# Sixteen-head attention with two heads in the halves of TensorE's rows, row and column scores side by side

## The chip, the cores and the metric

One core of one Trainium2 chip runs the whole program. The metric is the device time of one execution in microseconds (us); the kernel before took 780.82 us (median of 3 runs, 778.27 to 783.65). TensorE is called PE here, VectorE DVE, ScalarE ACT, GpSimd POOL and SyncE SP.

## The reference

Four layers, each an attention over a context and then a feed-forward part, every one added to `x` (8 batches of 256 tokens, 128 wide) after a layer norm:

```
x = x + L0_xattn(norm(x), ctx)   # att0: 8 heads of 16
x = x + L0_ffn(norm(x))          # ffn0: mixes each token with the one before it
x = x + L1_xattn(norm(x), ctx)   # att1: 16 heads of 8, then relu(out @ W1 + b1) @ W2 + b2
x = x + L1_ffn(norm(x))          # moe1: 8 experts, top 2
x = x + L2_xattn(norm(x), ctx)   # att2: 8 heads of 16
x = x + L2_ffn(norm(x))          # moe2
x = x + L3_xattn(norm(x), ctx)   # att3: one head
x = x + L3_ffn(norm(x))          # moe3: 8 experts, top 2, and a shared one
```

The change is in att1. Per batch and head it computes

```
scores = einsum("bnhd,bmhd->bhnm", q, k) / sqrt(8)       # 256 x 256 for each of 16 heads
out    = einsum("bhnm,bmhd->bnhd", softmax(scores), v)
h      = relu(out @ W1 + b1);  y = h @ W2 + b2
```

## The kernel before

Each engine has its own instruction stream, written out in order; semaphores alone tie them together, so an engine that waits holds up all that is written behind it. att0, ffn0 and att1 form one pipeline ("flow") over batches. A step of the flow has one batch in each role: `p` gets its queries and keys, `m` its row scores and maxima, `a` its column scores, exponentials and averages, `d` its output chain. Steps that hold an att1 batch in `m`, `a` or `d` have 16 **beats**. Tables of numbers say in which beat a piece is issued (`COL_BEAT`, `VALUE_BEAT`, `CHAIN_BEATS`, `SORT_STEPS` and so on).

Queries and keys are split into three bf16 parts, and SP copies them by DMA into a **stack**: for a head, the partitions hold the products of parts that are to be summed (`SLOTS`: nine products of 8 dimensions make 72 partitions in att1, padded to 96). A head's 256 x 256 scores are computed twice on PE, each time by two matmuls of 256 columns:

- `rows` (L2076): queries down the partitions; DVE takes each query's maximum (`negmax`, L952).
- `columns` (L2088): keys down the partitions; three more partitions of the stack carry the negative maxima, so that ACT (L1732) can take the exponential straight from PSUM.

Between them, for one batch: POOL splits the maxima in three (L1474 and on), PE turns them (`turn_max`, L2117), ACT copies them (`maxt`, L1798), and SP writes them into the stack by DMA (L787); the columns wait for that. `averages` (L2104) multiplies the exponentials of four heads by the values, four tiles of 32 columns of the array at a time; ACT copies the result (`nd`, L1737), PE turns it (`turn_averages`, L2128), DVE divides (L921, L924), PE turns that (`turn_o`, L2058), ACT copies it (`ot`, L1747), PE computes the hidden layer (L2171), ACT its relu (L1754), PE the output (L2202), and DVE adds it to `x` (L934). Three stacks are used in turn, so a batch's stack is written again three batches later.

In att1's steps each beat issues the columns of one head of `a`, then the rows of one head of `m`; other pieces of PE work stand between beats. From the last step on, pieces of moe1's routing for tiles 0 to 7 stand between them too (`SORT_STEPS["moe1"]`). moe1 then runs its 46 tiles of 128 tokens, about 1.45 us each.

Of the kernel before, what the change touches and what calls it, by code (L numbers as in the profile page):

```python
# [32 lines left out]
P = 128  # L33
B = 8
# [19 lines left out]
MAXROW = 96  # L54


# [34 lines left out]
def part_tiles(g):  # L91
# [13 lines left out]
    "moe1": {"stats": ((-1, 3), (2, 3)), "rstd": ((-1, 4), (2, 4)), "norm": ((-1, 8), (2, 6)),  # L105
             "turn": ((-1, 10), (-1, 12), (2, 13), (2, 15)), "turned": ((-1, 11), (-1, 13), (3, 0), (3, 1)),
             "logits": (-1, 15), "top": (0, 1), "pick": (0, 4), "mark": (0, 6), "exp": (0, 7), "rank": (0, 8),
             "place": (0, 9), "weigh": (1, 12), "load": (2, 6), "logits2": (3, 3)},
# [4 lines left out]
SEND_FROM = {"moe1": 12, "moe2": 7}  # L113
# [27 lines left out]
COL_BEAT = {8: 3, 16: 6}  # L141
GROUP_LAG = 5
VALUE_BEAT = 4
NORM_BEAT = {8: 4, 16: 7}
PLACE_BEAT = {8: 5, 16: 7}


MIX_BEATS = {"stats": (5, 5), "rstd": (6, 6), "norm": (7, 10), "turn": (3, 5), "turned": (4, 6), "rk": (6, 10), "gate": (7, 11),
             "gated": (5, 6), "mixed": (6, 7)}


CHAIN = ("turn", "finish", "turn_o", "ot", "proj", "hid", "proj2", "residual")
CHAIN_BEATS = {8: (1, 2, 4, 5, 6, None, None, 7), 16: (1, 2, 4, 5, 6, 7, 9, 10)}
# [131 lines left out]
def build(nc, args, out):  # L285
# [3 lines left out]
    with ExitStack() as ctx:  # L289
# [6 lines left out]
        stack_in = [ctx.enter_context(nc.semaphore(f"stack_in{i}")) for i in range(3)]  # L296
        maxrow_in = [ctx.enter_context(nc.semaphore(f"maxrow_in{i}")) for i in range(3)]
        const_ready = ctx.enter_context(nc.semaphore("const_ready"))
        maxrow_ones = ctx.enter_context(nc.semaphore("maxrow_ones"))
        rows_padded = ctx.enter_context(nc.semaphore("rows_padded"))  # L300
# [88 lines left out]
        def lists_of(s):  # L389

            return stack[buf("att" + s[3:], B - 3)]
# [75 lines left out]

        def batch_at(flow, g):

            stages = FLOWS[flow]  # L470
            last = B * len(stages)
            if g < 0:
                return stages[0], g
            return (stages[g // B], g % B) if g < last else (stages[-1], B + g - last)

        def steps_of(flow):
# [3 lines left out]
            last = B * len(FLOWS[flow])  # L480
            at = lambda g: batch_at(flow, g)
            for g in range(last + 4):
                p, m, a, d, n = (at(g - lag) for lag in (0, 1, 2, 3, -1))
                heads = max([H[s] for s, b in (m, a, d) if valid(b)], default=8)
# [22 lines left out]
        def group_beats(s):  # L507
            return [GROUP * j + COL_BEAT[H[s]] + GROUP_LAG for j in range(H[s] // GROUP)]

# [3 lines left out]
        def chain(link):  # L513


            def beats(s):
                k = CHAIN_BEATS[H[s]][CHAIN.index(link)]
                return [] if k is None or (s != "att1" and link in ("hid", "proj2")) else [region_beats(s)[-1] + k - H[s]]
            return beats

        def region_beats(s):
            per = H[s] // GROUP // REGIONS
            return [k + 1 for k in group_beats(s)[per - 1::per]]
# [73 lines left out]
        def uses(s, b):  # L597

            return [st for st in ATT for i in range(B)
                    if buf(st, i) == buf(s, b) and (ATT.index(st), i) <= (ATT.index(s), b)]  # L600

        def stack_total(s, b):

            return sum(16 * len(SLOTS[st]) for st in uses(s, b))
# [66 lines left out]
        def maxrow_total(s, b):  # L671
            return 16 * len(uses(s, b))
# [5 lines left out]
        def _(sp):  # L678
# [70 lines left out]
            def spread_heads(s, p):  # L749

                nh, dh, i = H[s], D // H[s], buf(s, p)
                if s == "att1" and p < 3:
                    sp.wait_ge(rows_padded, p + 1)
                    sp.wait_ge(rows_filled, 3)
                if (s, p) == EARLY:
                    wait(sp, "experts_ready", "moe1", 0)
                wait(sp, "cols_psum", s, p - 3)
                for j, (qa, kc) in enumerate(SLOTS[s]):
                    if j == 0:
                        wait(sp, "qk0_ready", s, p)  # L760
                    if j == 1:
                        wait(sp, "qk1_ready", s, p)
                    if j == 4:
                        wait(sp, "qk2_ready", s, p)
                    n = len(SLOTS[s])
                    sp.dma_start(stack[i][j:j + n * (dh - 1) + 1:n, 0:nh, :, :],
                                 qk_parts[:, qa:3 + kc + 1:3 + kc - qa, :]).then_inc(stack_in[i], 16)
# [1790 lines left out]
```

## Time and profile before

| | |
|---|---|
| median of 3 runs | 780.82 us |
| the profiled execution | 789.78 us |
| its span, first to last instruction | 788.0 us |
| busy: PE, DVE, ACT, POOL | 644.8, 483.9, 395.6, 303.8 us |
| row scores of att1, first to last batch (DVE's maxima) | 131.0 to 289.4 us |
| column scores of att1 end (ACT's exponentials) | 308.4 us |

Read the stretch from 131 to 308 us as nine steps of 18 to 23 us, each with one batch's 16 heads. In the timeline the column "idle before" says how long the engine had nothing running before the group, and what released it. Matmuls overlap one another: a matmul that lasts 0.27 us by its record can be followed by the next one 0.11 us after its start. So the distance from start to start is what a group costs PE, not its busy time.

### The profile page before, as it was taken

To read this page: it belongs to the slowest core of one execution; us is meant where nothing else is said; L and a number is where in the kernel's file an instruction comes from. 1 tells how busy PE (TensorE), PEld (TensorE's weight loads), DVE (VectorE), ACT (ScalarE), POOL (GpSimd) and SP (SyncE) were. 2 spreads that over 40 slices of the span, in tenths; PEclk is the share of its full clock that TensorE was granted. 3 is DMA by queue.
4 is the path that set the end of the run, shared out by engine and by line. 5 is a ranking of instruction groups with operands and counts; after the bars stand their busy time and mean duration, and the time that the engine had idled before them with its cause. 6 is when DMAs were issued, how large, how long until landed. Compare 5 with 4: busy or idle time off the path is not lost.

```text
span 788.0 us, 15312 instructions
## 1 busy us (share of the span) xinstructions
PE 644.8 (82%) x4712; PEld 471.8 (60%) x4712; DVE 483.9 (61%) x1396; ACT 395.6 (50%) x892; POOL 303.8 (39%) x456
## 2 busy tenths in 40 slices
PE   2698887899998887899977787747898677699997
PEld 1355665566665544799944555427787566356655
DVE  4567765877678553555867775636657655455543
ACT  5356574466666455466624655425676454132221
POOL 4435455433323036162756744372545730000000
PEclk9999999999999899699976998857999999699999
DMA  6254423333333100144354441012344200223331
GB/s 177 61 136 105 124 70 90 96 107 88 88 96 86 52 19 35 49 135 115 105 138 122 114 120 43 15 41 80 119 138 141 75 11 1 69 63 102 100 96 56
DMA packets 93575, 68.52 MB, mean 87 GB/s; under 512 B 9800, under 2 KB 84424, under 8 KB 93272
## 3 DMA queue, kind: packets, MB, share of 16 engines
q1 hardware_dynamic: 89400, 59.15, 26.9%
q0 software_dynamic: 4096, 8.40, 3.5%
q8 instruction: 40, 0.66, 0.4%
q14 instruction: 39, 0.32, 0.1%
HBM read 30.75 MB, written 14.35 MB: 57 GB/s over the span
## 4 chain that ended last, share of the span: by engine, by line
PE 35%; DVE 9%; issue 6%; DMA 5%; POOL 3%; ACT 2%; SPq 0%; DVEq 0%; ACTq 0%; POOLq 0%
PE ps L2389 6%; PE ps L2399 4%; PE ps L2427 4%; PE ps L2429 4%; PE ps L2440 4%; DMA late<-outputs_moe,placed 2%; DVE negmax L952 2%; PE ps L2076 1%; POOL gathered L1575 1%; PE ps L2028 1%; PE ps L2383 1%; PE ps L2104 1%; PE ps L2088 1%; DVE x_sb L1270 1%; POOL rstd L1441 1%
## 5 line engine op out<-in xcount | busy, mean ns | idle before, releaser
L952 DVE TENSOR_REDUCE negmax<-ps 128x2 f32<-128x512 f32 x256 | 169.2, 686 | 100.6 <-PE ps L2076 99.7
L1732 ACT ACTIVATE exps<-ps 128x512 f32<-128x512 f32 x256 | 148.9, 599 | 102.2 <-PE ps L2088 100.8
L2076 PE MATMUL ps<-stack 96*128 96x256 bf16 x512 | 103.7, 297 | 26.5 <-DVE negmax L952 22.6
L2088 PE MATMUL ps<-stack 99*128 99x256 bf16 x512 | 101.2, 288 | 19.8 <-DMA stack<-maxt 18.7
L1575 POOL DMA_INDIRECT gathered<-z,placed x64 | 62.6, 978 | 66.8 <-PE ps L2383 28.5
L2088 PEld LDWEIGHTS ps<-stack 99*128 99x128 bf16 x512 | 44.1, 102 | 62.1 <-DMA stack<-maxt 25.1
L1593 POOL DMA_INDIRECT late<-outputs_moe,placed x64 | 62.1, 971 | 49.2 <-PE ps L2383 14.8
L2076 PEld LDWEIGHTS ps<-stack 96*128 96x128 bf16 x512 | 48.6, 104 | 52.1 <-DVE negmax L952 38.5
L2104 PE MATMUL ps<-exps,values 128*32 128x256 f32 x1024 | 75.5, 413 | 1.2 <-ACT exps L1732 1.0
L1977 ACT ACTIVATE gated<-ps 128x512 f32<-128x512 f32 x36 | 21.5, 597 | 83.4 <-PE ps L2429 83.4
L2399 PE MATMUL ps<-pack_moe,ht 128*128 x368 | 59.4, 285 | 1.5 <-DVE y_kept L1357 0.6
L1377 DVE TENSOR_TENSOR ht<-ps,gated 128x512 f32<-128x512 f32 x36 | 24.9, 692 | 45.2 <-ACT gated L1977 45.1
L2399 PEld LDWEIGHTS ps<-pack_moe,ht 128*128 128x128 f32 x368 | 49.1, 194 | 4.6 <-issue 3.1
L2389 PE MATMUL ps<-gated,exps 128*128 128x128 f32 x368 | 51.1, 284 | 0.1
L2440 PEld LDWEIGHTS ps<-pack_moe,ht 128*128 128x128 f32 x288 | 38.2, 195 | 20.3 <-issue 13.4
L2389 PEld LDWEIGHTS ps<-gated,exps 128*128 128x128 f32 x368 | 47.1, 200 | 0.6 <-issue 0.4
L2104 PEld LDWEIGHTS ps<-exps,values 128*32 128x32 f32 x1024 | 30.7, 114 | 21.3 <-issue 9.3
L2440 PE MATMUL ps<-pack_moe,ht 128*128 128x128 f32 x288 | 39.3, 280 | 3.2 <-DVE ht L1377 3.2
L2427 PE MATMUL ps<-stack,pack_moe 128*128 128x512 f32 x64 | 33.8, 611 | 7.0 <-DVE stack L1400 7.0
L1520 POOL TENSOR_TENSOR qk_rest<-qk,qk_parts 128x512 f32<-128x512 f32 x24 | 27.7, 1154 | 29.9 <-DVE qk_parts L963 29.9
L2429 PE MATMUL ps<-stack,pack_moe 128*128 128x512 f32 x64 | 33.6, 607 | 0.0
L1963 ACT ACTIVATE ht<-ps,pack_moe 128x128 f32<-128x128 f32 x92 | 28.7, 364 | 9.5 <-PE ps L2399 6.9
(224 smaller groups left out, 1267.5 us busy)
## 6 DMA issues: line engine op xcount, KB each, us to landing
stack<-qk_parts SPq DMA_DIRECT2D x168, 128.0 KB
stack<-weights_t SPq DMA_DIRECT2D x32, 256.0 KB, 3.3
outputs_moe<-y_kept SPq DMA_DIRECT2D x92, 64.0 KB
ht<-gathered SPq DMA_DIRECT2D x44, 128.0 KB, 2.2
pack_moe<-in_moe SPq DMA_DIRECT2D x11, 256.5 KB, 3.9
pack_moe<-in_moe SPq DMA_DIRECT2D x6, 429.5 KB
gathered<-y_kept SPq DMA_DIRECT2D x10, 256.0 KB, 3.4
pack_moe<-in_moe SPq DMA_DIRECT2D x1, 1732.0 KB, 7.4
```

What stands on the lines that cost most here:

```text
L952: dve.tensor_reduce(negmax_of[b % 2][:, :, h:h + 1].rearrange("p t h -> p (t h)"), ps[:, h % 2, :].rearrange("p (t k) -> p t k", t=2), AX, ...
L1575: pool.indirect_dma_start(gathered[g], at, z[:, t, :], None).then_inc(sent[i], 16)
L1593: pool.indirect_dma_start(back[:, n, :], None, averaged[s, g], at).then_inc(back_in[n], 16)
L1732: nc.scalar.activation(exps[:, i, :], ps[:, 2 + h % 2, :], ACT.Exp, scale=scale)\
L2076: last = pe.matmul(ps[:, h % 2, t * T:(t + 1) * T], st[0:MAXROW, h, 0, t * P:(t + 1) * P], st[0:MAXROW, h, 1, :], start=True, stop=True)
L2088: last = pe.matmul(ps[:, 2 + h % 2, t * T:(t + 1) * T], st[0:MAXROW + 3, h, 1, t * P:(t + 1) * P], st[0:MAXROW + 3, h, 0, :], start=True, ...
L2104: last = pe.matmul(ps[STRIP * k:STRIP * (k + 1), AV, r * T:(r + 1) * T], values[nh][:, buf(s, a), kt, u, :], exps[:, slot(s, a, u), kt * T ...
L2389: last = pe.matmul(ps[:, (j + 1) % 2, c * P:(c + 1) * P], up_kept[s][:, (j + 1) % 2, c * P:(c + 1) * P], taken_t[:, (j + 1) % 2, :], start ...
L2399: last = pe.matmul(ps[:, 3 + (j - 1) % 2, 0:D], turned[:, (j - 1) % 2, c * P:(c + 1) * P], par(s, "experts")[:, bass.ds(at + (up_width(s) ...
L2427: pe.matmul(ps[:, 2 * (i % 2), :], par(s, "w1")[:, w * P:(w + 1) * P], rhs, start=True, stop=True)
L2429: pe.matmul(ps[:, 2 * (i % 2) + 1, :], par(s, "w3")[:, w * P:(w + 1) * P], rhs, start=True, stop=True).then_inc(sem["up_psum"], 1)
L2440: last = pe.matmul(ps[:, 4 + blk % 2, t * D:(t + 1) * D], ht[:, q % 2, 0, t * P:(t + 1) * P], par(s, "w2")[:, w * P:(w + 1) * P], start=(q ...
```

## The change

What it does, part by part:

1. att1's stack keeps six of the nine products: 48 partitions a head. Even heads lie in partitions 0 to 47, odd heads in 64 to 111, and their three rows of maxima behind them. The matmuls of rows and columns thereby use tiles of 64 rows of the array (half the array) in place of all 128 rows. One of SP's DMAs serves one half, so there are 12 of 64 KB per batch instead of 9 of 128 KB, and two for the maxima instead of one.
2. In each beat that has a column head and a row head of att1, which then lie in different halves, PE issues column, row, column, row (`rows_beside_columns`), after both waits.
3. `COL_BEAT` of att1 goes from 6 to 8. Averages come in two halves in two neighbouring beats, and so do hidden layer and output; the output chain's beats are further apart, and it ends 8 beats later. The values' matmul goes from beat 4 to 12.
4. A fourth home for att1's stacks: a head pair needs one slot, so the third stack holds two batches.
5. The padding changes: POOL's three clears of the stack (L1544) go; ACT writes ones into the unused partitions in two smaller pieces per home, for the fourth home in att1's third step, beat 10; ACT writes the ones of the maxima's rows (`fill_ones`) for 8 head slots instead of 16, and a fourth time at moe1's tile 5.
6. moe1's routing of the first tiles comes later: its statistics go from beat 3 to beat 11 of the step with tail -1, its places from beat 9 to beat 12 of the next.

```diff
-    "att1": [(0, 0), (0, 1), (1, 0), (1, 1), (0, 2), (2, 0), (1, 2), (2, 1), (2, 2)],
+    "att1": [(0, 0), (0, 1), (1, 0), (1, 1), (0, 2), (2, 0)],
-MAXROW = 96
+MAXROW = {"att0": 96, "att1": 48, "att2": 96}
+HALF = P // 2
+HALVES = {"att0": 1, "att1": 2, "att2": 1}
...
-    "moe1": {"stats": ((-1, 3), (2, 3)), "rstd": ((-1, 4), (2, 4)), "norm": ((-1, 8), (2, 6)),
+    "moe1": {"stats": ((-1, 11), (2, 11)), "rstd": ((-1, 12), (2, 12)), "norm": ((-1, 14), (2, 15)),
...
-COL_BEAT = {8: 3, 16: 6}
-GROUP_LAG = 5
-VALUE_BEAT = 4
+COL_BEAT = {8: 3, 16: 8}
+GROUP_LAG = {8: 5, 16: 6}
+GROUP_BEATS = {8: 1, 16: 2}
+VALUE_BEAT = {8: 4, 16: 12}
...
-CHAIN = ("turn", "finish", "turn_o", "ot", "proj", "hid", "proj2", "residual")
-CHAIN_BEATS = {8: (1, 2, 4, 5, 6, None, None, 7), 16: (1, 2, 4, 5, 6, 7, 9, 10)}
+CHAIN = ("turn", "finish", "turn_o", "ot", "proj", "proj_b", "hid", "proj2", "proj2_b", "residual")
+CHAIN_BEATS = {8: (1, 2, 4, 5, 6, None, None, None, None, 7), 16: (1, 2, 5, 5, 8, 9, 10, 12, 13, 14)}
...
+        def home(s, b):
+            if s == "att1":
+                return 3 + b % HOMES, stack[min(b % HOMES, 2)], 8 * (b % HOMES < 3)
+            return buf(s, b), stack[buf(s, b)], 0
...
+            def spread_slot(s, p, j):
+                nh, dh, (i, st, first), n = H[s], D // H[s], home(s, p), len(SLOTS[s])
+                qa, kc = SLOTS[s][j]
+                for half in range(HALVES[s]):
+                    at = half * HALF + j
+                    sp.dma_start(st[at:at + n * (dh - 1) + 1:n, first:first + nh // HALVES[s], :, :],
+                                 qk_parts[half::HALVES[s], qa:3 + kc + 1:3 + kc - qa, :]).then_inc(stack_in[i], 16)
...
-                            wait(pool, "cols_psum", s, p - 3)
-                            pool.memset(stack[buf(s, p)][0:MAXROW, 0:8, 1, :].bitcast(F32), 0.0).then_inc(rows_padded, 1)
...
+            def row_half(s, m, h, t):
+                (at, k), (_, st, first) = half_place(s, h), home(s, m)
+                st = st[at:at + MAXROW[s], first + k, :, :]
+                return pe.matmul(ps[:, h % 2, t * T:(t + 1) * T], st[:, 0, t * P:(t + 1) * P], st[:, 1, :], start=True, stop=True)
...
+            def rows_beside_columns(s, a, h, m, g):
+                wait_columns(s, a, h)
+                wait_rows(s, m, g)
+                for t in range(2):
+                    column = column_half(s, a, h, t)
+                    row = row_half(s, m, g, t)
+                column.then_inc(sem["cols_psum"], 1)
+                row.then_inc(sem["rows_psum"], 1)
...
-                for kt in range(2):
+                for kt in halves:
...
+                if [st for st, _, _ in col + row] == ["att1", "att1"] and (col[0][2] + row[0][2]) % 2:
+                    rows_beside_columns(*col[0], *row[0][1:])
```

PE's stream in the middle of att1, where averages, `turn_o` and the hidden layer stand between the beats. Before (L2088 columns, L2076 rows, L2104 averages of four heads, L2058 `turn_o`, L2171 hidden layer):

```order
L2104 MATMUL ps<-exps,values16 32x256 x8
L2088 MATMUL ps<-stack2 128x256 x2
L2076 MATMUL ps<-stack0 128x256 x2
L2058 MATMUL ps<-pack_consts,o 128x128 x2
L2088 MATMUL ps<-stack2 128x256 x2
L2076 MATMUL ps<-stack0 128x256 x2
L2088 MATMUL ps<-stack2 128x256 x2
L2076 MATMUL ps<-stack0 128x256 x2
L2171 MATMUL ps<-ot,pack_att1 128x256 x2
```

The same place in the changed kernel (L2146 columns, L2133 rows, L2184 averages, L2197 `turn_max`, L2203 hidden layer):

```order
L2184 MATMUL ps<-exps,values16 32x256 x4
L2146 MATMUL ps<-stack2 128x256
L2133 MATMUL ps<-stack1 128x256
L2146 MATMUL ps<-stack2 128x256
L2133 MATMUL ps<-stack1 128x256
L2197 MATMUL ps<-ident16,negmax_parts 48x128 x2
L2184 MATMUL ps<-exps,values16 32x256 x4
L2146 MATMUL ps<-stack2 128x256
L2133 MATMUL ps<-stack1 128x256
L2146 MATMUL ps<-stack2 128x256
L2133 MATMUL ps<-stack1 128x256
L2203 MATMUL ps<-ot,pack_att1 128x256
```

Columns and rows now alternate matmul by matmul, and in such a step a piece of other work follows every beat's four matmuls, where before some beats followed one another with nothing between.

The same stream where the averages' last group of a batch is followed by `turn_averages`, which needs ACT's copy of it. Before (L2128 `turn_averages`):

```order
L2104 MATMUL ps<-exps,values16 32x256 x8
L2088 MATMUL ps<-stack1 128x256 x2
L2076 MATMUL ps<-stack2 128x256 x2
L2088 MATMUL ps<-stack1 128x256 x2
L2076 MATMUL ps<-stack2 128x256 x2
L2128 MATMUL ps<-pack_consts,nd 128x128 x4
```

In the changed kernel (L2277 values, L2219 `turn_averages`):

```order
L2184 MATMUL ps<-exps,values16 32x256 x4
L2146 MATMUL ps<-stack2 128x256
L2133 MATMUL ps<-stack0 128x256
L2146 MATMUL ps<-stack2 128x256
L2133 MATMUL ps<-stack0 128x256
L2277 MATMUL ps<-pack_att1,ctxt_sb 128x128 x2
L2146 MATMUL ps<-stack2 128x256
L2133 MATMUL ps<-stack0 128x256
L2146 MATMUL ps<-stack2 128x256
L2133 MATMUL ps<-stack0 128x256
L2219 MATMUL ps<-pack_consts,nd 128x128 x4
```

Two beats lie between as before, with the values' matmuls now among them.

SP's stream in one step of att1. Before (L787 the maxima of one batch, L766 the stack of the next but one, L730 and L695 loads for later):

```order
L787 DMA stack1<-maxt 3x16x256
L766 DMA stack0<-qk_parts 8x32x256 x5
L766 DMA stack0<-qk_parts 8x16x512
L766 DMA stack0<-qk_parts 8x32x256 x3
L730 DMA gathered_1<-y_kept 128x4x128
L695 DMA pack_moe<-in_moe1 128x513
```

In the changed kernel (L814 maxima, L781 stack):

```order
L781 DMA stack0<-qk_parts 8x16x256 x2
L814 DMA stack2<-maxt 3x8x256 x2
L781 DMA stack0<-qk_parts 8x16x256 x8
L781 DMA stack0<-qk_parts 8x8x512 x2
L756 DMA gathered_1<-y_kept 128x4x128
L721 DMA pack_moe<-in_moe1 128x513
```

Two DMAs of the stack now stand ahead of the maxima, and 14 DMAs take the place of 10.

## Rows read from the trace of the kernel before

**Rows 1.** The page, part 1: busy time, share of the span, instructions.

```profile
span 788.0 us, 15312 instructions
PE 644.8 (82%) x4712; PEld 471.8 (60%) x4712; DVE 483.9 (61%) x1396; ACT 395.6 (50%) x892; POOL 303.8 (39%) x456
```

**Rows 2.** Windows by att1's steps: busy us and instructions of each engine, PE clock.

```profile
core 0: us, PE busy (x) PEld busy (x) DVE busy (x) ACT busy (x) POOL busy (x), PEclk, DMA share, GB/s
131.00:149.20 18.20, 16.68 (x142) 11.51 (x139) 14.43 (x34) 8.80 (x23) 6.34 (x10) 0.91 0.35 97
149.20:168.30 19.10, 15.89 (x131) 10.51 (x132) 14.07 (x35) 9.87 (x25) 8.72 (x17) 1.00 0.33 92
168.30:188.00 19.70, 17.97 (x170) 12.33 (x168) 14.09 (x32) 13.51 (x32) 7.54 (x15) 1.00 0.33 89
188.00:207.80 19.80, 18.78 (x178) 13.35 (x178) 13.45 (x27) 13.55 (x33) 6.65 (x13) 1.00 0.32 89
225.90:243.90 18.00, 16.31 (x160) 10.96 (x159) 12.38 (x23) 12.22 (x28) 4.47 (x9) 1.00 0.30 82
243.90:267.30 23.40, 20.48 (x178) 13.78 (x177) 15.83 (x45) 13.22 (x29) 5.95 (x9) 0.90 0.26 67
267.30:289.40 22.10, 18.41 (x161) 11.50 (x161) 15.96 (x42) 10.69 (x24) 4.25 (x8) 0.88 0.09 26
289.40:308.40 19.00, 14.20 (x144) 7.72 (x143) 4.88 (x24) 13.36 (x27) 11.51 (x18) 1.00 0.10 37
```

**Rows 3.** Timeline of PE in one step: start, us, line, shape, [idle before <- releaser].

```profile
...
193.54 0.38 PE L2076 MATMUL ps<-stack 96*128 96x256 bf16 x2
193.76 0.38 PE L2088 MATMUL ps<-stack 99*128 99x256 bf16 x2
193.98 0.38 PE L2076 MATMUL ps<-stack 96*128 96x256 bf16 x2
194.29 1.07 PE L2104 MATMUL ps<-exps,values 128*32 128x256 f32 x16
195.30 0.39 PE L2088 MATMUL ps<-stack 99*128 99x256 bf16 x2
...
206.31 0.59 PE L2144 MATMUL ps<-zt,pack_att 128*128 128x256 f32 x2
206.75 0.60 PE L2145 MATMUL ps<-ctxt_sb,pack_att 96*128 96x256 f32 x2
```

**Rows 4.** Timeline of PE, cut at 194.53 us: the first four matmuls of a group.

```profile
194.29 0.42 PE L2104 MATMUL ps<-exps,values 128*32 128x256 f32 x4
```

**Rows 5.** Waits from 188 to 244 us: engine, line, releaser: us, times, longest.

```profile
PE ps L2088 <- DMA stack<-maxt: 1.6, 3, 0.9
...
PE ps L2171 <- ACT ot L1747: 1.2, 3, 0.4
PE ps L2128 <- ACT nd L1737: 1.2, 3, 0.4
```

**Rows 6.** The same view from 243.9 to 289.4 us.

```profile
PE ps L2076 <- DVE negmax L952: 2.4, 3, 1.0
PE ps L2088 <- DMA stack<-maxt: 2.3, 2, 1.4
PE ps L2171 <- ACT ot L1747: 1.0, 2, 0.8
```

**Rows 7.** Timeline of SP's queue in the same step.

```profile
190.51 0.77 SPq L787 DMA_DIRECT2D stack<-maxt  x1
192.24 6.41 SPq L766 DMA_DIRECT2D stack<-qk_parts  x9
```

**Rows 8.** Groups by line, whole span: ACT's fills.

```profile
L1678 ACT ACTIVATE stack<-zt 32x2048 f32<-32x2048 f32 x3 | 5.7, 1906 | 0.1
L1685 ACT ACTIVATE stack<-neghalf 3x2048 f32<-3x2048 f32 x3 | 5.5, 1893 | 0.0
```

**Rows 9.** Timeline of PE around the end of att1.

```profile
294.52 0.61 PE L2088 MATMUL ps<-stack 99*128 99x256 bf16 x4 [1.72 <-DMA stack<-maxt]
...
326.99 0.23 PE L2355 MATMUL ps<-picks,upper 128*128 128x64 bf16 x1 [1.50 <-DVE picks L1217]
```

More of the change, by code:

```diff
@@ L389, in lists_of @@
         def lists_of(s):
[L391 removed]
+            return home("att" + s[3:], B - 3)[1]
         picks16 = sb("picks16", [P, len(PART[0]), E], BF16)
@@ L476, in steps_of @@
         def steps_of(flow):
-            last = B * len(FLOWS[flow])
+            stages = FLOWS[flow]
+            last = B * len(stages)
             at = lambda g: batch_at(flow, g)
@@ L764, in spread_heads, with place_maxima @@
                         wait(sp, "qk2_ready", s, p)
-                    n = len(SLOTS[s])
-                    sp.dma_start(stack[i][j:j + n * (dh - 1) + 1:n, 0:nh, :, :],
-                                 qk_parts[:, qa:3 + kc + 1:3 + kc - qa, :]).then_inc(stack_in[i], 16)
+                    spread_slot(s, p, j)
+            def spread_heads(s, p):
+                spread_first(s, p)
+                spread_rest(s, p)
+            def place_maxima(s, m):
+                wait(sp, "maxt_ready", s, m)
+                wait(sp, "cols_psum", s, freed(s, m))
+                i, st, first = home(s, m)
+                for half in range(HALVES[s]):
+                    at = half * HALF + MAXROW[s]
+                    sp.dma_start(st[at:at + 3, first:first + H[s] // HALVES[s], 0, :], maxt[half:3 * H[s]:HALVES[s], :])\
+                        .then_inc(maxrow_in[i], 16)
             for flow in FLOWS:
@@ new lines, in wait_columns, with column_half @@
+            def wait_columns(s, a, h):
+                if h == 0:
+                    pe.wait_ge(maxrow_in[home(s, a)[0]], maxrow_total(s, a))
+                    pe.wait_ge(maxrow_ones, min(a + 1, 3) if s == "att0" else 3 if s == "att1" else 4)
+                wait(pe, "exp_ready", s, a, h - 2)
+            def column_half(s, a, h, t):
+                (at, k), (_, st, first) = half_place(s, h), home(s, a)
+                st = st[at:at + MAXROW[s] + 3, first + k, :, :]
+                return pe.matmul(ps[:, 2 + h % 2, t * T:(t + 1) * T], st[:, 1, t * P:(t + 1) * P], st[:, 0, :], start=True, stop=True)
@@ L2113, in turn_max @@
                 wait(pe, "placed_ready", "moe1", 0, 0) if (s, m) == ("att1", B - 1) else None
-                wait(pe, "route_exp_in", "moe1", 0, 0) if (s, m) == ("att1", B - 2) else None
                 rows_of = 3 * H[s]
@@ L2119, in turn_max, with find_hidden, find_output @@
                 last.then_inc(sem["maxt_psum"], 1)
+            def find_hidden(s, c):
+                return pe.matmul(ps[:, TURN, c * T:(c + 1) * T], par(s, "w1")[:, c * P:(c + 1) * P], ot[:, :], start=True, stop=True)
+            def find_output(s, t):
+                for c in range(2):
+                    last = pe.matmul(ps[:, ND, (2 + t) * D:(3 + t) * D], hid[:, c, t * P:(t + 1) * P],
+                                     par(s, "w2")[:, c * P:(c + 1) * P], start=(c == 0), stop=(c == 1))
+                return last
             def turn_averages(s, d):
@@ L2152, in beat @@
                     wait(pe, "qk_ready", s, p)
+                    wait(pe, "hid_ready", sd, d - 1) if sd == "att1" and valid(d - 1) else None
                 if u == mix_at("turn", heads) and f2 is not None:
@@ L2215, in beat @@
                     wait(pe, "qk_ready", s, p)
+                    wait(pe, "hid_ready", sd, d - 1) if sd == "att1" and valid(d - 1) else None
                     wait(pe, "val_ready", "ffn0", f2) if f2 is not None else None
@@ L2236, in beat @@
                 for st, b, j in due(flow, step, u, "a", group_beats):
-                    averages(st, b, j)
+                    averages(st, b, j, range(3 - GROUP_BEATS[H[st]]))
+                for st, b, j in due(flow, step, u, "a", later_halves):
+                    averages(st, b, j, (1,))
             def attention(flow):
```

196 lines of the change are left out of this document (107 added, 89 removed).

## The prediction

> **What bounds the kernel now.** I read the page's first part, then the windows by step, then PE's timeline inside one step, then the waits, and last the end of att1.
>
> PE is busy 82% of the span and no other engine over 61% [rows 1], but that is a mean over different stages. The windows cut att1 at its steps [rows 2]. In the four steady steps, from 168.3 to 243.9 us, a step takes 18.0 to 19.8 us; PE is busy for 16.3 to 18.8 of it, DVE for 12.4 to 14.1 and ACT for 12.2 to 13.6, at the full clock (2.4 GHz). So PE bounds them, with some 4 us of room to the next engine. From 243.9 to 289.4 the steps are longer, 23.4 and 22.1 us, with a granted clock of 0.90 and 0.88 and DVE at 16: routing work of moe1 stands in them. In the last step, columns only, ACT has 13.4 of 19.0.
>
> The timeline gives what PE pays [rows 3]. Groups of two score matmuls start 0.22 us apart, so one costs 0.11 us, and a step's 64 of them 7.0 us. A step has four groups of averages; a group's 16 matmuls take 1.01 us to the next one's start. Two float32 matmuls of 256 columns over the whole array take 0.44 us, 0.22 each, and so 16 of them would take 3.5; four averages in the four column strips fit into 0.42 us by their records [rows 4]. So tiles of the array do run beside one another here, for columns. Entering such a group costs extra: the last rows start at 193.98, are done with their 0.22 at 194.20, and the averages start at 194.29, which makes **0.09 us** per change of tile shape. Leaving may cost 0.13 (1.01 less four times 0.22), but that rests on a modelled pitch.
>
> The waits of three steady steps are few [rows 5]: 1.6 us for the maxima's DMA, 1.2 each for `ot` and `nd`, 4.0 us in all, 1.3 a step. In the two longer steps they are 2.3 for the DMA, 1.0 for `ot` and 2.4 for DVE's maxima [rows 6].
>
> **The change, part by part.**
>
> *Halves.* In a beat with a column and a row head, four matmuls in sequence (0.44 us) become two pairs. If the halves run beside each other, a pair costs 0.11 and the beat 0.22: a gain of 0.22 x 16 = 3.5 us per steady step. No tile of 64 rows stands in this trace; the two bounds are 0.22 us per beat (like the strips) and 0.44 (like two whole-array matmuls). I take 0.22, since the nearest row is that of the strips.
>
> *Changes of tile shape.* Before, a step entered and left a special shape four times, 8 changes. After, each of 16 beats' pairs is followed by work of another shape, 32 changes: 24 more. At 0.09 us that is +2.2 us a step. The bounds are 0 (half rows need no change) and 0.13 each, +3.1.
> The Trainium skill, "TensorEngine Tiling (Array Packing)", section Key Properties, says that changing the tiling mode, not just the tile, drains TensorE. The 0.09 us fits it for column strips, and no row here shows it for halves. It speaks against this change, since the beats were spread apart by other work.
>
> *Waits.* Columns now come 5 beats after the turn of the maxima instead of 3, and `turn_averages` and the hidden layer stand further from what they need: the 1.3 us a step go [rows 5]. SP works longer for this: a maxima DMA occupies its queue for 0.77 us and nine of the stack 6.41, 0.71 each [rows 7]. Fourteen at 0.71 to 0.77 are 9.9 to 10.8 us, two of them ahead of the maxima; this fits into a step of 16 us, so I cost it at nothing. If it did not fit, the maxima would be late and the columns would wait as in the last step now, 1.72 us [rows 9]. The joint wait of a pair is new: row and column now stand still if either DVE or ACT is late. In the steady steps PE waits for neither at a score matmul [rows 5]. With the steps shorter I take +0.5, between 0 and the 1.3 just removed.
>
> A steady step: -3.5 + 2.2 - 1.3 + 0.5 = **-2.1 us**, four of them -8.4.
>
> *The two longer steps.* The same, with 3.3 us of DMA and `ot` waits in two steps, 1.65 each, in place of 1.3 [rows 6]: -3.5 + 2.2 - 1.65 + 0.5 = -2.45 each, **-4.9**. Routing now has 17 beats in place of 22; if DVE's waits of 2.4 us double, half of this is lost, and if they go it is -7.3.
>
> *Before and after the steady steps.* From 149.2 to 168.3 nine beats are paired: 9 x 0.22 = 2.0 saved, up to 18 more changes x 0.09 = 1.6 paid. ACT has to write the fourth home, as the fills of 1906 ns a piece [rows 8], but is busy for only 9.9 of 19.1 us; I take +0.1 and call the step **-0.3**. From 131.0 to 149.2 the rows of att1 in halves stand alone among att0's columns over the whole array: no pair, some 14 round trips of 0.18, +2.5. PE has 1.5 us idle there, part of which takes it: **+2.0** (0 to 2.5). In the last step the columns start two beats later, about 1.7 us by its 0.85 a beat (columns and two groups of averages in a step of 19.0 us over 22 beats), and the DMA wait of 1.72 goes [rows 9]; in halves and alone, they also pay changes: **+0.5**. From there to routing's rank matmul at 326.99, which waits for DVE's picks [rows 9], and on to moe1, the chain's steps are the same. At moe1's tile 5 ACT writes ones for 8 slots; half of 1893 ns [rows 8] on a chain from PE through ACT, bounds 0 and 0.95: **+0.5**. POOL's clears free POOL, which bounds nothing here. The filling of the homes at the start lies beside loads: 0.
>
> Sum: -8.4 - 4.9 - 0.3 + 2.0 + 0.5 + 0.5 = **-10.6**, say -10 us. The profiled execution took 789.8 us, so it would take 780; the median of the runs shown is 780.8, 9 us below the profiled one, and the forecast for a median is **771 us**.
>
> **The rivals.** A measurement of this kernel can tell about 1% from no change, here 773.0 to 788.6.
>
> *Halves cost no change of shape.* Then 24 x 0.09 = 2.2 us more are gained in six steps, 13 us, and 2 in the step at 131: **756 us**. For it: rows and columns both use all 128 columns, so the output side does not change. Against it: the gap seen before averages. By the skill's rule named above this rival falls away; a gap of 0.09 us ahead of strips is the only row that bears on it.
>
> *The saved time goes back to DVE and ACT.* Each head passes through DVE once and ACT once, both take other work between, and two buffers of scores each (the remainder of the head by two) are all that stands between them and PE. If pairs wait for both, the six steps keep their length, the step at 131 pays its 2: **781 us**, no change. For it: DVE's 12.4 to 14.1 busy plus lumps of other work in one beat. Against it: 4 us of room per step [rows 2], and the lumps are split.
>
> *Slower: the halves run one after another.* The place is the pair. If its second matmul waits for the first, 105 beats (6 x 16 + 9) cost 0.44 in place of 0.22 while the changes are paid: 105 x 0.22 = 23 us more than forecast, **793 us**. It decides from a price per beat of 0.22 + 10/105 = 0.32 us on. For it: no tile of 64 rows in the trace. Against it: the strips of the averages [rows 4].
> The Trainium skill, "TensorE: Matmul & The Clock Gate", Part 3, gives a measured speedup of 3.07 for four row tiles of 32 rows; by it this rival falls. No row here shows row tiles.
>
> **How the numbers follow.** Forecast (765 to 777): 0.46. No cost of shape: 0.22. Back to DVE and ACT: 0.15. One after another: 0.13. The rest, 0.04, is a collapse of the order, such as SP late for every step. The range takes in the forecast, the second rival with 7 us above it, up to 788, and the first rival with 2 below it, down to 754; outside lie the serial halves, the rest and what of the first rival gains more. Faster by over 1% needs less than 773: some two thirds of the forecast's own range (0.31) and the first rival, 0.53. Within 1%: the forecast's other third and the second rival, 0.32. Slower: 0.15.
>
> **What would show it.** In the changed profile's timeline of PE the second matmul of a pair starts about 0.01 us after the first, and two pairs are 0.11 us apart; starts 0.11 us apart within a pair mean serial halves. A gap of 0.09 us or so ahead of and behind each beat's pairs shows the changes of shape; without it the first rival is right. The steady steps should last 16 to 17.7 us, PE still with the fewest idle time, no wait of columns on the maxima's DMA, of `turn_averages` on `nd` or the hidden layer on `ot`. If instead pairs wait for `negmax` or `exps` in most beats, the second rival is right. The forecast is wrong too if SP's maxima land after the columns' beat, if the granted clock falls in the steady steps, or if routing's places come so late that moe1 starts later than att1's end allows.

## The result and the profile after

The changed kernel takes **792.26 us** (median of 4 runs, 788.16 to 793.07), the kernel before 782.24. The ratio is 1.0106 (95% interval 1.0071 to 1.0141), so it is slower by 1.1%, where 10 us less had been forecast; 792 also lies outside the range. A second series gave 1.0092 (1.0056 to 1.0128).

PE is busy for 651.0 us, 82% of the span, and the other engines are within 3 us of what they were [rows 1].

The kernel before was profiled once more, in an execution of 786.29 us, nearer its median than the one that the prediction rests on. Its windows, by stretches of steps (start and end in us, their length, busy us and instructions of PE, PE's weight loads, DVE, ACT and POOL, PE's granted clock as a share of 2.4 GHz, DMA share, GB/s):

```profile
128.00:146.20 18.20, 16.73 (x142) 11.59 (x140) 14.56 (x35) 8.87 (x23) 6.40 (x10) 0.91 0.36 98
146.20:165.20 19.00, 15.87 (x130) 10.50 (x131) 13.98 (x35) 9.78 (x25) 8.62 (x17) 1.00 0.33 92
165.20:240.80 75.60, 69.95 (x667) 48.23 (x665) 53.33 (x109) 51.98 (x119) 24.71 (x46) 1.00 0.32 88
240.80:286.30 45.50, 38.89 (x337) 25.29 (x336) 31.79 (x86) 23.91 (x52) 10.20 (x16) 0.89 0.18 47
286.30:305.30 19.00, 14.17 (x144) 7.69 (x142) 4.86 (x24) 13.34 (x27) 11.49 (x18) 1.00 0.10 37
305.30:398.70 93.40, 84.19 (x685) 79.59 (x685) 56.98 (x214) 50.24 (x110) 42.96 (x48) 0.93 0.35 99
```

The same stretches of the changed kernel, which answer to [rows 2] (the fourth line is a part of the third, its last three steps):

```profile
126.20:155.20 29.00, 23.71 (x142) 11.78 (x142) 14.99 (x35) 9.56 (x24) 6.04 (x9) 0.76 0.18 47
155.20:174.60 19.40, 18.55 (x112) 10.37 (x112) 14.17 (x33) 10.46 (x23) 7.34 (x14) 0.65 0.26 69
174.60:243.00 68.40, 65.60 (x659) 31.13 (x656) 53.53 (x109) 51.70 (x115) 26.48 (x49) 1.00 0.28 74
191.70:243.00 51.30, 50.05 (x497) 23.47 (x497) 39.32 (x78) 39.13 (x87) 18.85 (x35) 1.00 0.27 72
243.00:288.00 45.00, 40.17 (x339) 18.76 (x342) 32.14 (x86) 24.75 (x53) 9.37 (x16) 0.77 0.14 38
288.00:308.40 20.40, 18.86 (x166) 7.55 (x167) 3.31 (x10) 15.84 (x33) 12.41 (x17) 1.00 0.10 38
308.40:407.00 98.60, 86.96 (x692) 82.32 (x690) 58.69 (x226) 51.30 (x111) 42.61 (x49) 0.90 0.33 94
```

Read the length, the number behind the two ends of each line, against its partner. The sums are 270.7 and 280.8 us. The two profiled spans differ by less, 784.5 and 789.7. One reason stands just ahead of the first stretch, which begins with att1's first maximum. In the first profile PE's line there was

```profile
130.52 0.39 PE L2076 MATMUL ps<-stack 96*128 96x256 bf16 x2 [2.65 <-DMA stack<-qk_parts]
```

(2.40 us in the second): att1's first rows waited for the DMA of their stack. In the changed kernel this wait is gone. From att0's last rows to att1's first maximum it takes 6.2 us (120.02 to 126.19) where the kernel before took 8.6 (119.36 to 128.00), so 2.5 us were gained that no term of the forecast had. What took the wait away was not tried; it stays away in the runs below. The other reason is that this execution was 3.1 us shorter behind moe1, where the change has no part.

| stretch | forecast | measured |
|---|---|---|
| ahead of the first step, rows' wait for their stack | 0 | -2.5 |
| first step, rows of att1 beside att0's columns | +2.0 | **+10.8** |
| second step, 9 beats paired | -0.3 | +0.4 |
| four steady steps | -8.4 | **-7.2** |
| two steps with routing | -4.9 | -0.5 |
| columns only | +0.5 | +1.4 |
| end of att1 and moe1 | +0.5 | **+5.2** |
| sum | -10.6 | +7.6 |

The steady steps do most of what was forecast. The loss stands in the first step and behind att1; the two steps with routing gain almost nothing.

Two rows of the table compare unequal work, since columns, averages and the output chain now come some beats later. The second step has 112 of PE's matmuls in place of 130, and the first of the steady steps lacks a hidden layer and an output; later steps take this over, the columns-only step with 166 in place of 144. The last three steady steps hold the same work in both kernels: they went from 55.9 us (188.0 to 243.9 in [rows 2]) to 51.3, which is 1.5 us a step.

**The steady steps.** PE's timeline in the changed kernel, beside [rows 3] (L2146 columns, L2133 rows; columns: start, us, line, shape, count):

```profile
208.04 0.27 PE L2146 MATMUL ps<-stack 51*128 51x256 bf16 x1
208.04 0.27 PE L2133 MATMUL ps<-stack 48*128 48x256 bf16 x1
208.24 0.64 PE L2184 MATMUL ps<-exps,values 128*32 128x256 f32 x8
208.81 0.28 PE L2146 MATMUL ps<-stack 51*128 51x256 bf16 x1
...
208.93 0.27 PE L2146 MATMUL ps<-stack 51*128 51x256 bf16 x1
```

Column and row start together, and the next pair 0.12 us later: four score matmuls cost 0.23 us where two took 0.22 before. The averages start 0.20 after the last pair, 0.09 more than its 0.11; eight of them, two groups of four at 0.22, take 0.57 to the next pair, 0.13 more than 0.44. So each change of shape costs about 0.1 us in both directions. The Trainium skill, "TensorEngine Tiling (Array Packing)", section Key Properties, has this drain on a change of tiling mode, and the trace agrees. With float32 work of the whole array between the pairs it is more: four matmuls of L2277 stand at 205.41, 0.20 after the last pair, and the next pair at 206.05, 0.64 later, where the same four took 0.44 before (191.38 to 191.82). That makes 0.29 us for entering and leaving, against 0.22 with averages.

The waits of PE from 175 to 243 us, four steps, beside [rows 5] (line, releaser: us, times, longest):

```profile
PE ps L2146 <- DVE negmax L998: 1.3, 3, 0.7
...
PE ps L2146 <- ACT exps L1781: 0.3, 1, 0.3
```

The waits for the maxima's DMA, `nd` and `ot` are gone; pairs wait for DVE and ACT 1.6 us in four steps, 0.4 a step where 0.5 was taken. The line left out is 1.1 us of idle time ahead of L2253 in two steps, which the profile puts down to no wait ("issue").

**The first step.** PE's wait there; before, columns waited 0.55 us here:

```profile
131.31 0.46 PE L2146 MATMUL ps<-stack 99*128 99x256 bf16 x2 [4.24 <-DMA stack<-maxt]
```

SP's queue (start, us) shows why, beside [rows 7]:

```profile
127.30 1.62 SPq L781 DMA_DIRECT2D stack<-qk_parts  x2
129.02 0.77 SPq L814 DMA_DIRECT2D stack<-maxt  x1
```

and DVE and ACT what SP's two entries needed:

```profile
124.68 0.37 ACT L1849 ACTIVATE maxt<-ps 24x256 bf16<-24x256 bf16 x1
126.80 0.42 DVE L1009 CAST qk_parts<-qk 128x512 bf16<-128x512 f32 x1
```

The maxima of att0's last batch were ready at 125.05. They were sent at 129.02, because SP stood at the two stack parts written ahead of them, and these need DVE's cast, done at 127.22. The columns waited 4.24 us for that. In the same place the clock falls (windows of 4 us; PEclk stands behind POOL's count):

```profile
132.00:136.00 4.00, 4.00 (x26) 1.82 (x24) 2.20 (x5) 1.00 (x2) 0.00 (x0) 0.50 0.38 100
...
140.00:144.00 4.00, 4.00 (x24) 2.25 (x26) 2.48 (x6) 1.69 (x4) 0.00 (x0) 0.50 0.00 0
```

PE is idle from 127.1 to 131.3, and from 132 to 144 it runs at 1.2 GHz although it is busy all the time.

**The end.** PE behind att1's last averages, beside [rows 9] (brackets: idle before, and what ended it; L2072 turns moe1's normed tiles, L2203 is the hidden layer, L2082 routing's logits, L2208 the output, L2458 the rank):

```profile
314.61 0.85 PE L2072 MATMUL ps<-pack_consts,z 128*128 128x128 f32 x6 [2.01 <-DVE z L944]
315.32 1.56 PE L2203 MATMUL ps<-ot,pack_att 128*128 128x256 f32 x4
316.67 2.57 PE L2082 MATMUL ps<-pack_moe,zt 128*128 128x8 f32 x12
319.09 2.06 PE L2208 MATMUL ps<-pack_att,hid 128*128 128x128 f32 x8
...
330.18 0.23 PE L2458 MATMUL ps<-picks,upper 128*128 128x64 bf16 x1 [1.49 <-DVE picks L1263]
```

The last hidden layer stands behind a turn that waits 2.01 us for DVE, and the output behind twelve logits matmuls of 2.4 us. From the last averages (309.02) to the rank it is 21.2 us; before, 18.5.

### The profile page after: what moved, and what is told of

It is laid out like the page before. It is cut to its first block, busy times and chain, and to the rows that moved or that the text cites. A ratio compares the mean times of both kernels' runs of the same rounds, so it can differ in the third digit from the quotient of the medians.

```text
span 789.7 us, 15455 instructions
## 1 busy us (share of the span) xinstructions
PE 651.0 (82%) x4712; PEld 445.5 (56%) x4712; DVE 484.4 (61%) x1396; ACT 398.0 (50%) x898; POOL 301.5 (38%) x453
## 4 chain that ended last, share of the span: by engine, by line
PE 33%; DVE 9%; issue 6%; DMA 4%; POOL 4%; ACT 3%; SPq 1%; DVEq 0%; ACTq 0%; POOLq 0%
PE ps L2492 6%; PE ps L2530 4%; PE ps L2532 4%; PE ps L2543 4%; PE ps L2502 3%; POOL gathered L1617 2%; DVE negmax L998 2%; DMA late<-outputs_moe,placed 2%; PE ps L2082 1%; DVE x_sb L1316 1%; PE ps L2133 1%; PE ps L2184 1%; PE ps L2146 1%; PE ps L2486 1%; PE ps L2385 1%
## 5 line engine op out<-in xcount | busy, mean ns | idle before, releaser
L2133 PE MATMUL ps<-stack 96*128 96x256 bf16 (+1 forms) x512 | 106.7, 306 | 22.7 <-DVE negmax L998 20.9
L2146 PE MATMUL ps<-stack 99*128 99x256 bf16 (+1 forms) x512 | 103.5, 294 | 19.9 <-DMA stack<-maxt 15.5
L2146 PEld LDWEIGHTS ps<-stack 99*128 99x128 bf16 (+1 forms) x512 | 38.0, 100 | 82.6 <-issue 39.0
L2184 PE MATMUL ps<-exps,values 128*32 128x256 f32 x1024 | 81.9, 415 | 0.2 <-issue 0.2
L2133 PEld LDWEIGHTS ps<-stack 96*128 96x128 bf16 (+1 forms) x512 | 39.4, 102 | 46.2 <-DVE negmax L998 34.8
L2530 PE MATMUL ps<-stack,pack_moe 128*128 128x512 f32 x64 | 33.9, 611 | 6.9 <-DVE stack L1446 6.9
L2184 PEld LDWEIGHTS ps<-exps,values 128*32 128x32 f32 x1024 | 27.0, 113 | 22.0 <-issue 15.6
L1511 POOL TENSOR_TENSOR xb<-x_sb,pack_att 128x256 f32<-128x256 f32 x24 | 16.2, 673 | 59.4 <-DVE x_sb L980 38.0
```

The source lines that it names most:

```text
L2133: return pe.matmul(ps[:, h % 2, t * T:(t + 1) * T], st[:, 0, t * P:(t + 1) * P], st[:, 1, :], start=True, stop=True)
L2146: return pe.matmul(ps[:, 2 + h % 2, t * T:(t + 1) * T], st[:, 1, t * P:(t + 1) * P], st[:, 0, :], start=True, stop=True)
L2184: last = pe.matmul(ps[STRIP * k:STRIP * (k + 1), AV, r * T:(r + 1) * T], values[nh][:, buf(s, a), kt, u, :], exps[:, slot(s, a, u), kt * T ...
L2530: pe.matmul(ps[:, 2 * (i % 2), :], par(s, "w1")[:, w * P:(w + 1) * P], rhs, start=True, stop=True)
```

## The experiments

Times are medians; the ratio is that to the kernel before in the same series, and across series it is the safer reading.

**The kernel before again.** No edit.

> The kernel before once more, for a trace beside those of the others. If the profile that the prediction rests on is typical, the maxima of att1's first batch begin near 131 us and its last exponential ends near 308 us, and the granted clock is at its lower level for some 14 us between 120 and 310 us; a whole time near 782 us would then say that the 8 us between the profiled 789.8 us and the median lie behind att1.

786.29 us in one run. Its windows are shown above. Its stretches of att1 are as long as in the first profile to 0.1 us, so the rows that the prediction rests on were typical; what the first profiled execution took longer lay elsewhere. The whole time was not near the 782 us that the expectation names.

**SP's order.**

```diff
-                    if spreads and sm == "att1":
+                    if spreads and sa == "att1":
                         spread_first(s, p)
                     if valid(a):
                         place_maxima(sa, a)
                     if spreads:
-                        spread_rest(s, p) if sm == "att1" else spread_heads(s, p)
+                        spread_rest(s, p) if sa == "att1" else spread_heads(s, p)
```

> The changed kernel, but in the one step that has att0's last batch in role a, SP copies its maxima ahead of the next batch's first stack part. Theory A (a wait and no more): PE's 4.24 us wait at 127 us goes down to about 0.5 and the time falls by 3 to 4 us against the changed kernel's 792, to about 788.5. Theory B (the idle time also brings the clock down, which halves the 13.65 us behind it): the stretch at the lower clock from 131.5 us goes as well and the time falls by 8 to 11 us, to about 783. Theory C (matmuls on half the rows hold the clock down by themselves): the wait goes, the clock falls at 131 or soon behind it all the same, and the time is about 789.

778.91 us, ratio 0.9939 (0.9905 to 0.9973): 13 us less than the changed kernel, above the 8 to 11 of theory B, so theories A and C are too small by far. PE's wait, and the windows of the first two steps:

```profile
129.55 0.39 PE L2146 MATMUL ps<-stack 99*128 99x256 bf16 x2 [0.36 <-DMA stack<-maxt]
```

```profile
128.30:147.50 19.20, 17.81 (x142) 9.75 (x142) 14.69 (x34) 9.46 (x24) 6.05 (x9) 1.00 0.27 71
147.50:166.30 18.80, 17.65 (x112) 10.23 (x112) 14.17 (x33) 10.47 (x23) 7.34 (x14) 0.73 0.27 72
```

The wait is 0.36 in place of 4.24, and the step 19.2 us in place of 29.0, at the full clock. Of the 9.8 us, 3.9 are the wait. What goes beyond theory B lies mainly in the two steps with routing, 42.1 us here where the changed kernel had 45.0.

**The wait kept, but filled.** In the changed kernel, ahead of the same wait:

```diff
+                if (s, a, h) == ("att0", B - 1, 0):
+                    wait(pe, "exp_ready", s, a, h - 2)
+                    for i in range(72):
+                        pe.matmul(ps[:, 2 + h % 2, 0:P], ident16[:, :], ident16[:, :], start=True, stop=True)
                 if h == 0:
                     pe.wait_ge(maxrow_in[home(s, a)[0]], maxrow_total(s, a))
```

> The changed kernel (792 us) with SP's order as it is, so with the wait of 4.24 us for the maxima; but ahead of that wait PE runs 72 extra matmuls of 128 columns on the whole array, 4.0 us by 0.055 each, whose results are overwritten. Nothing that the kernel needs comes earlier. If the idle time is what brings the clock down at 131.5 us, the 13.65 us at the lower level go and the time falls by 4 to 9 us, to 783 to 788. If half rows bring the clock down by themselves, or if the loss was the wait alone, it stays at 790 to 794.

780.64 us, ratio 0.9973 (0.9935 to 1.0010), against 791.21 of the changed kernel in the same series (ratio 1.0092): 10.6 us less by the medians, 9.3 by the ratios, where 4 to 9 were expected, with 72 matmuls more and nothing sooner. The extra work in PE's timeline, and the window of the step:

```profile
127.97 4.19 PE L2140 MATMUL ps<-ident 128*128 128x128 bf16 x72
```

```profile
127.20:149.90 22.70, 21.71 (x214) 13.72 (x213) 14.62 (x34) 9.37 (x24) 6.05 (x9) 1.00 0.22 59
```

The step takes 22.7 us: 3.5 more than with the maxima first, and 6.3 less than with the wait left empty. So the 29.0 us divide into 19.2 for the step, 3.5 for the wait, and 6.3 for the clock that fell at its end. The second step is 1.7 us shorter too, 17.7 us at a granted clock of 0.81 against 19.4 at 0.65.

**The changed kernel again**, in the series of the filler. No edit.

> The changed kernel once more, beside the run with the filler: 789 to 793 us, with the wait of some 4.2 us near 127 us and the lower clock behind it.

791.21 us, as expected.

**The end of att1.** Two edits of `SORT_STEPS["moe1"]`, first on top of the maxima first, then alone:

```diff
-             "turn": ((-1, 15), (0, 2), (3, 2), (3, 3)), "turned": ((0, 0), (0, 3), (3, 3), (3, 4)),
+             "turn": ((-1, 15), (0, 2), (3, 6), (3, 7)), "turned": ((0, 0), (0, 3), (3, 7), (3, 8)),
...
-             "place": (0, 12), "weigh": (1, 12), "load": (2, 6), "logits2": (3, 6)},
+             "place": (0, 12), "weigh": (1, 12), "load": (2, 6), "logits2": (3, 10)},
```

> As the run with the maxima first, and besides the turns of moe1's tiles 8 to 13 stand behind att1's last hidden layer on PE (beats 6 and 7 of the last step instead of 2 and 3), and their logits behind its output (beat 10 instead of 6). If these two insertions are what lengthened the end of att1, the rank matmul comes 3 to 4 us sooner behind the last averages, and the time falls by 3 to 5 us more against the run before it. If the end was longer for the clock alone, nothing changes.

774.00 us, ratio **0.9864** (0.9825 to 0.9904), 4.9 us less than the run before it. PE at the end of att1:

```profile
305.04 1.10 PE L2203 MATMUL ps<-ot,pack_att 128*128 128x256 f32 x4 [0.66 <-ACT ot L1796]
306.40 0.85 PE L2072 MATMUL ps<-pack_consts,z 128*128 128x128 f32 x6 [0.26 <-DVE z L944]
307.08 1.14 PE L2208 MATMUL ps<-pack_att,hid 128*128 128x128 f32 x8
...
317.27 0.24 PE L2458 MATMUL ps<-picks,upper 128*128 128x64 bf16 x1 [1.50 <-DVE picks L1263]
```

The twelve logits matmuls follow the output (at 308.08). From the last averages (300.80) to the rank it is now 16.5 us, 4.7 less than in the changed kernel and 3.8 less than in the run before it (297.86 to 318.11). Part of the 4.7 is the clock again: the output's eight matmuls take 1.14 us here and 2.06 there.

> The changed kernel with only the turns of moe1's tiles 8 to 13 and their logits moved behind the hidden layer and the output. If the two repairs are independent, this one is worth what it was behind the other, 778.9 - 774.0 = 4.9 us: 785 to 789. If the end of att1 is only hurt by the clock, 790 to 793.

784.56 us, ratio 1.0011 (0.9982 to 1.0041), against 791.21 in the same series: 6.7 us less, 6.3 by the ratios. The two repairs add up: 13.1 and 6.3 us alone by the ratios, 18.9 together.

**The order of a pair.** In the changed kernel:

```diff
                 for t in range(2):
                     column = column_half(s, a, h, t)
+                for t in range(2):
                     row = row_half(s, m, g, t)
```

> The changed kernel with column, column, row, row in each paired beat instead of column, row, column, row; waits and all else unchanged. If matmuls of different halves run beside each other only when they are neighbours in the stream, two matmuls of one half follow each other at 0.11 us and the neighbours in the middle overlap: a beat costs 0.33 in place of 0.22 us, 105 beats 11.6 us, of which a part is covered by waits for DVE: 797 to 804 us. If the halves gained nothing, 792.

790.05 us, ratio 1.0100 (1.0062 to 1.0138): no difference to the changed kernel. That is the number of the theory that halves gain nothing, and still not its proof, for the matmuls overlapped all the same. The stream holds column, column, row, row; the trace shows

```profile
207.84 0.28 PE L2146 MATMUL ps<-stack 51*128 51x256 bf16 x1
207.85 0.28 PE L2133 MATMUL ps<-stack 48*128 48x256 bf16 x1
207.96 0.27 PE L2146 MATMUL ps<-stack 51*128 51x256 bf16 x1
207.97 0.27 PE L2133 MATMUL ps<-stack 48*128 48x256 bf16 x1
```

The first row starts beside the first column and 0.11 us ahead of the second column, which stands before it in the stream. By these records each half works through its own matmuls. The Trainium skill, "TensorE: Matmul & The Clock Gate", Part 3, says that matmuls start and end in the order of the program; these starts differ from it, and the records decide here.

**Column and row in the same half**, on the kernel of 774.00 us:

```diff
-COL_BEAT = {8: 3, 16: 8}
+COL_BEAT = {8: 3, 16: 9}
```

> The kernel of the run with the turns late (774.0 us), with att1's columns one beat later (COL_BEAT 9 in place of 8), so that the column head and the row head of a beat lie in the same half of the rows. Every tile, wait and change of shape is as before; only the matmuls cannot run beside each other. The theory that this is where the gain comes from: a beat costs 0.44 us in place of 0.22, 105 beats 23 us, less what waits cover, so 785 to 797 us, and the steady steps last about 3 us longer. If the gain comes from the shorter waits alone: 774 to 776.

832.84 us, ratio 1.0626 (1.0587 to 1.0666). PE's timeline at the full clock, and the windows of the first steady step and of all four:

```profile
207.42 0.39 PE L2146 MATMUL ps<-stack 51*128 51x256 bf16 x2
207.65 0.38 PE L2133 MATMUL ps<-stack 48*128 48x256 bf16 x2
```

```profile
166.60:186.10 19.50, 17.86 (x163) 9.62 (x164) 14.31 (x32) 12.68 (x29) 7.09 (x12) 1.00 0.26 70
166.60:263.20 96.60, 90.26 (x659) 47.05 (x660) 53.82 (x109) 52.27 (x115) 25.64 (x47) 0.82 0.20 52
```

The two heads of a beat cost 0.23 us and the same again, as forecast for serial halves. The step at full clock is 19.5 us where the changed kernel has 17.1 for the same batch (174.6 to 191.7), 2.4 more. The time rises by 59 us, not by up to 23. The rest stands where the clock is lower: the four steady steps take 96.6 us at a granted clock of 0.82 where the kernel of 774.00 us has 68.4 at 1.00, and the mean over the profiled execution is 0.866 against 0.921. What brings it down in the steady steps was not tried; waits for `nd` and `exps` of up to 0.7 us stand there.

**A change of shape more.** On the kernel of 774.00 us, and the control with `ident16` cut to the half of the row head:

```diff
                 for t in range(2):
+                    if t:
+                        pe.matmul(ps[:, g % 2, T:T + 8], ident16[0:P, :], ident16[0:P, 0:8], start=True, stop=True)
                     column = column_half(s, a, h, t)
```

> The same kernel (774.0 us) with one extra matmul of 8 columns on the whole array between the two pairs of each of the 105 paired beats; its result is overwritten. If a change of tile shape costs about 0.09 to 0.13 us each, two more per beat cost 19 to 27 us, less what waits cover: 787 to 801 us, and the two pairs of a beat start 0.35 us apart in place of 0.11. If halves need no change of shape, only the matmul itself counts, some 0.03 to 0.05 us a beat: 777 to 779.

813.42 us, ratio 1.0372 (1.0328 to 1.0416), 39 us more where 13 to 27 were expected. The timeline:

```profile
207.43 0.28 PE L2133 MATMUL ps<-stack 48*128 48x256 bf16 x1
207.64 0.18 PE L2167 MATMUL ps<-ident 128*128 128x8 bf16 x1
207.75 0.28 PE L2146 MATMUL ps<-stack 51*128 51x256 bf16 x1
```

> The control: the same extra matmul of 8 columns, but on the half of the array in which the beat's row head lies, so without a change of tile shape. Both theories: 0.03 to 0.05 us a beat, 777 to 779 us.

785.66 us, with runs from 771.02 to 792.09: by its whole time this decides nothing. The timeline does, and the windows of the four steady steps, first on the whole array, then on the half:

```profile
208.36 0.27 PE L2146 MATMUL ps<-stack 51*128 51x256 bf16 x1
208.36 0.17 PE L2168 MATMUL ps<-ident 64*128 64x8 bf16 x1
208.39 0.27 PE L2133 MATMUL ps<-stack 48*128 48x256 bf16 x1
```

```profile
165.30:246.90 81.60, 80.37 (x723) 42.48 (x722) 54.21 (x109) 52.50 (x115) 25.81 (x48) 0.98 0.23 62
164.40:233.80 69.40, 66.89 (x724) 37.15 (x720) 53.91 (x109) 51.77 (x115) 26.89 (x48) 1.00 0.28 73
```

On the whole array the small matmul puts the pairs 0.32 us apart in place of 0.11, so two changes cost 0.21 with it. On the half it delays its row by 0.03. That is the price that the forecast had. The steady steps, 68.4 us without the extra matmul, bear it out: on the whole array they take 13.2 us more, 3.3 a step, as 16 beats at 0.21 give; on the half 1.0 more. The time of the first run beyond 105 x 0.21 = 22 us lies behind them: its two steps with routing take 52.8 us at a granted clock of 0.69, where the kernel of 774.00 us has 45.0 at 0.77, and the stretch from there to moe1's end 126.5 at 0.82 against 113.6 at 0.95.

**Filler in the rows' step**, on the kernel of 774.00 us:

```diff
                     for st, b, h in row:
+                        if st == "att1" and not col:
+                            wait_rows(st, b, h)
+                            for i in range(6):
+                                pe.matmul(ps[:, h % 2, 0:P], ident16[:, :], ident16[:, :], start=True, stop=True)
                         rows(st, b, h)
```

> The same kernel (774.0 us) with six extra matmuls of 128 columns on the whole array, 0.33 us, ahead of each of att1's row heads that stand in a beat without columns (the stretch from 128 to 155 us); their results are overwritten. If PE's idle time there, waiting for DVE, is what brings the clock down at 150.3 us for 10 us, the clock stays up, and the time falls by 2 to 4 us. If rows on half the array bring it down, the clock falls all the same and the time rises by 3 to 6 us, for the added work and its changes of shape.

775.01 us, ratio 0.9885 (0.9849 to 0.9922): no gain. The windows of the first two steps:

```profile
126.50:147.70 21.20, 20.87 (x187) 12.41 (x187) 14.87 (x34) 9.81 (x25) 6.43 (x11) 1.00 0.25 64
147.70:164.70 17.00, 15.92 (x148) 9.43 (x148) 14.22 (x34) 10.04 (x23) 6.80 (x13) 1.00 0.30 80
```

The clock stays up. The filler closes the idle time, and it is also work on the whole array, so this run alone does not separate the two theories; half rows at the full clock in the steady steps, and in this first step with the maxima first, speak for the idle time. The second step is 17.0 us where the kernel without filler took 19.0, and the first 21.2 where it took 19.1, for the filler itself: the first theory was right about the clock, and the sum is nothing.

## Why the prediction was wrong

- **What bounds the kernel** held: PE bounds the steady steps, which went from 75.6 to 68.4 us.
- **Halves**: right. A beat's scores take 0.23 us where 0.22 was taken, and 0.45 when they share a half. The third rival named serial halves; the time did come out on its side, for other reasons.
- **Changes of shape**: right in kind, about 0.1 us each, seen at every beat and doubled in a run of its own; somewhat more in size, since work of the whole array between pairs costs 0.29 for both changes. The first rival (no cost) is out.
- **Waits in the steady steps**: right, those named went, and 0.4 us a step of new ones came. The second rival, time given back to DVE and ACT, is out.
- **The sum for a steady step** was -1.5 in place of -2.1 in the three steps of equal work. PE's idle time there fell from 3.9 to 1.3 us, 0.9 a step, where 0.8 was taken; its busy time from 52.0 to 50.1, 0.6 a step. An estimate from this: with 3.4 saved by the pairs (16 beats at 0.21), the changes took 2.8 a step where 2.2 was taken.
- **SP: wrong, and the first failure.** "[T]his fits into a step of 16 us, so I cost it at nothing" counted how long SP's entries last, for the steady steps alone. Two stack parts ahead of the maxima also make the maxima wait for what those parts wait for. In the first step of att1 this is DVE's cast, and a wait of 4.24 us came. The steady steps were costed rightly: there SP's fourteen entries took 9.5 us (within 192.79 to 202.49) and no column waited for the maxima. The prediction named a late DMA as a possibility, with 1.72 us, and did not look at the one step where the queue's head has another producer.
- **The clock: no term at all.** That wait cost its 3.5 us and 6.3 more, because the clock fell to 1.2 GHz at its end and stayed there for 12 us of full work and more. The prediction listed a falling clock as what would make it wrong, "in the steady steps", where it did not fall.
- **The end: wrong, the second failure.** "From there to routing's rank matmul [...] the chain's steps are the same" compared the steps of the chain and not what stands between them in PE's stream. Two moves of the table, which part 6 of the change does not list (`turn` to beats 2 and 3 of the last step, `logits2` from beat 3 to 6), put a waiting turn ahead of the last hidden layer, and 2.4 us of logits ahead of the output: 5 to 7 us by the two runs that took them away. With the orders put right this stretch is -0.1, so of the +0.5 for ACT's ones (1.05 us long, at 340.36) nothing is seen in the time.
- **The first step without these faults** is 19.2 us, +1.0 where +2.0 was taken. The second is 18.8, -0.2 for -0.3, but by luck: at the full clock, with filler ahead of its rows, it took 17.0, so a gain of 2.0 (with 18 matmuls fewer) was eaten by the clock. The columns-only step was +1.4 for +0.5.
- **The two routing steps**: forecast -4.9; measured -0.5 in the changed kernel with the granted clock at 0.77, where the kernel before had 0.89. This is a third miss, and its cause stays open. With the maxima first it was -3.4 (42.1 us at 0.84), and 42.1 at 0.84 too with the turns late alone; the kernel with both repairs had 45.0 us at 0.77. So in these four runs the steps are shorter where the clock fell less, and that does not follow the repairs. What decides it was not tried.
- **The wait that went unforeseen**, of att1's first rows for their stack: -2.5 us, no term.

With both faults repaired the ratio is 0.9864, 10.6 us less of 782.6 (8.6 by the medians), from a kernel that is the change with one condition and five beat numbers altered. That this is the size of the forecast is in part luck. In its trace the terms are: -2.5 ahead of the first step, then +0.9, 0.0, -7.2 in the steady steps, -0.5 with routing, +1.3 in the columns-only step and -0.1 at the end, -8.1 in all. The gain that nobody forecast stands in for a part of the one that routing did not give. The gain of the pairs was read rightly, and two orders were not read.

## What to carry to other kernels

When a step of a queue is moved ahead of another, what is queued behind inherits its wait: look for the one place, often the first or last round of a pipeline, where its producer is another than in the steady state. Compare the written orders of every engine on the critical end, not the list of its links. And price an idle time of PE with the clock behind it: here 3.5 us of waiting cost 6.3 us more, and 4.2 us of useless matmuls in the same gap won 9 to 11 in all.

## What the runs showed of the hardware

- Column and row matmuls on the two halves of the rows overlapped in full, 0.11 to 0.12 us a pair, whether they alternated in the stream or stood two and two.
- Entering or leaving a tile shape cost 0.09 to 0.13 us, between halves and strips as between strips and the whole array; an excursion from halves to four float32 matmuls on the whole array cost 0.29 us in both directions together. Two changes and a bf16 matmul of 8 columns cost 0.21 us, the same matmul without a change 0.03.
- After the idle time at 128 to 131 us the clock was at 1.2 GHz until past 144 us, although PE was busy for all of 132 to 144; with the gap filled, or closed, that step ran at 2.4 GHz throughout.
